# A hand-written order for every engine in the third stage of a fused four-layer network, and eight slots of reciprocals

## The reference, cut to what matters

```python
x = x + L2_attn(layernorm(x))   # 16 heads of 8, window of +-32, softmax, W_o
x = x + L2_ffn(layernorm(x))    # silu(x @ wg.T) * (x @ wu.T) @ wd.T, hidden 384
x = x + L3_attn(layernorm(x))   # 16 heads of 8, rope, latent k and v, causal by pages of 32
x = x + L3_ffn(layernorm(x))    # 8 experts, top 1; the router's part lies in this stage
```

```python
# L3_attn, per head
scores = einsum(q, k) / sqrt(8); scores[masked] = -inf
out = softmax(scores) @ v
```

## Time and profile before

| what | us |
|---|---|
| median of 3 runs | 1353.43 |
| lowest and highest | 1347.26, 1355.87 |
| the profiled execution | 1362.73 |
| span of its instructions | 1360.9 |
| rounds of the third stage from the second `l2f_0` (at 660.7) to the last (at 1127.5) | 76.1, 77.3, 78.7, 78.8, 79.8, 76.1 |
| from the last `l2f_0` to the stage's end at 1245 | 117.5 |

### The profile page before, as it was taken

The page is one execution under the profiler, slowest core; times in us unless marked ns, Lnnn a source line. Parts: engine busy times, 40 slices in busy tenths (PEclk is TensorE's granted clock), DMA queues, the critical chain, the costliest instruction groups (busy, mean ns, idle before and its releaser), DMA issues.

```text
span 1360.9 us, 39674 instructions
## 1 busy us (share of the span) xinstructions
PE 1117.9 (82%) x17027; PEld 805.4 (59%) x17027; DVE 823.8 (61%) x2399; ACT 567.4 (42%) x993; POOL 446.1 (33%) x538
## 2 busy tenths in 40 slices
PE   6999968888875798587888888888888887987895
PEld 4777737777764375354555656556565654553784
DVE  7587765667885122356758586776848575734332
ACT  3322102555452131324373745638274553451342
POOL 3233342344464154213131324133222403112565
PEclk9999979998985899899999999999999998998998
DMA  9455425543040421222112212202221200201784
GB/s 363 165 200 196 180 76 171 168 141 115 26 155 25 111 62 43 58 59 60 50 51 60 59 50 60 60 28 59 60 58 50 61 12 12 56 19 50 194 193 92
DMA packets 85169, 126.08 MB, mean 93 GB/s; under 512 B 14465, under 2 KB 66050, under 8 KB 84578
## 3 DMA queue, kind: packets, MB, share of 16 engines
q1 hardware_dynamic: 68258, 106.47, 24.8%
q0 software_dynamic: 10928, 13.64, 4.2%
q10 hardware_dynamic: 5808, 3.43, 1.0%
HBM read 50.82 MB, written 46.74 MB: 72 GB/s over the span
## 4 chain that ended last, share of the span: by engine, by line
PE 34%; DVE 26%; issue 13%; ACT 12%; POOL 6%; DMA 5%; SPq 1%; another core or an unknown queue 1%; PEldq 1%; ACTq 0%; DVEq 0%; PEld 0%; POOLq 0%
DVE mx L1712 9%; ACT MW L1996 6%; DVE bst L1144 2%; DVE mx L1703 2%; PE ps L996 2%; PE ps L987 2%; POOL xs L2134 2%; DMA MW<-l_moe_dram 2%; PE ps L797 1%; PE ps L988 1%; DVE X L1172 1%; POOL rr L2197 1%; PE ps L1110 1%; POOL rst L2080 1%; PE ps L909 1%
## 5 line engine op out<-in xcount | busy, mean ns | idle before, releaser
L1712 DVE TENSOR_REDUCE mx<-ps 128x2 f32<-128x1024 f32 (+3 forms) x176 | 188.6, 1119 | 30.8 <-PE ps L1033 30.6
L1996 ACT ACTIVATE MW<-ps 128x1024 f32<-128x1024 f32 x160 | 154.4, 1038 | 65.1 <-PE ps L1050 52.8
L2134 POOL DMA_INDIRECT xs<-xr,sidu x96 | 96.1, 1001 | 132.2 <-DVE sidu L1303 95.2
L2077 POOL TENSOR_SCALAR rst<-bmv 128x4 f32<-128x4 f32 x64 | 15.8, 247 | 293.5 <-DVE bmv L1147 292.9
L1065 PE MATMUL ps<-MW,Vp 128*16 128x128 f32 x2560 | 88.1, 279 | 4.6 <-ACT MW L1996 4.0
L1033 PE MATMUL ps<-K,Q 64*128 64x512 bf16 (+3 forms) x512 | 60.0, 303 | 18.2 <-DVE mx L1712 12.0
L1983 ACT ACTIVATE MW<-ps 128x1024 f32<-128x1024 f32 x64 | 63.5, 1026 | 27.1 <-PE ps L958 25.1
L1065 PEld LDWEIGHTS ps<-MW,Vp 128*16 128x16 f32 x2560 | 64.1, 98 | 16.2 <-ACT MW L1996 5.6
L2160 POOL DMA_INDIRECT out_dram<-qf,toku x39 | 60.6, 1555 | 37.1 <-DVE toku L1768 28.2
L1801 ACT COPY XT<-ps 128x512 f32<-128x512 f32 x48 | 28.2, 587 | 97.1 <-PE ps L617 78.7
L1703 DVE TENSOR_REDUCE mx<-ps 128x8 f32<-128x768 f32 x64 | 57.9, 948 | 14.6 <-PE ps L935 14.2
(11 more groups left out here) (377 smaller groups left out, 2676.6 us busy)
## 6 DMA issues: line engine op xcount, KB each, us to landing
xs<-hb SPq DMA_DIRECT2D x52, 528.0 KB, 8.9
MW<-l_moe_dram SPq DMA_DIRECT2D x19, 768.0 KB
MW<-l_moe_dram SPq DMA_DIRECT2D x20, 578.0 KB
Q<-spl SPq DMA_DIRECT2D x48, 128.0 KB
Q<-spm SPq DMA_DIRECT2D x48, 128.0 KB
K<-spl SPq DMA_DIRECT2D x43, 128.0 KB
K<-spm SPq DMA_DIRECT2D x43, 128.0 KB
MW<-l_moe_dram SPq DMA_DIRECT2D x16, 256.0 KB
```

The source lines that it names most:

```text
L1712: V.tensor_reduce(out=mx[1][:, :, s0:s0 + ns, t], in_=p.rearrange("p (e n) -> p e n", e=2)[:, :, 0:ns * nk].rearrange("p e (s k) -> p e s ...
L1996: A.activation(P3[k % 2][:, 1024 * half:1024 * half + 1024], p, ACT.Exp).then_inc(drained[u], 1)
L2134: G.indirect_dma_start(out=xs[L], out_offset=bass.IndirectOffsetOnAxis(ap=sidu[:, 4 * b + t:4 * b + t + 1], axis=0), in_=src[:, t, :], in_ ...
```

## The change

Two edits. `STEPS2` and `lanes(STEPS2, 74.5)` go, and `ORDER2` is written out with `sequences`: one list per engine, in which the n-th appearance of a name is batch n-1. Every (piece, batch) pair of before is in the new lists once and on the same engine; PE's list has 672 entries, DVE's 472, ACT's 320, POOL's 104, SP's 40. The pattern no longer repeats exactly from batch to batch. The slots of the PSUM ring follow PE's new order. Extra matmuls that a piece brings along (`AHEAD_OF`, and the ones in front of the last batch's `l3_m`) stay with their piece. The second edit gives `rden` 8 x 16 columns in place of 4 x 16, so that each of the four `_t` pieces of a batch has a slot of its own; in the old kernel `t0` and `t2` shared one.

```diff
-STEPS2 = [
-    ("l2_get", dict(SP=-130)),
...
-    ("l3t_x", dict(POOL=480.36)),
-]
-ORDER2 = lanes(STEPS2, 74.5)
+ORDER2 = sequences({
+    "PE": """
+        l2a_n l2_q l2_v l2a_n l2_m0 l2_m1 l2_m2 l2_m3 l2_n2 l2_q l2_e0 l2_e1 l2_o0 l2_e2 l2_o1 l2_t0 l2_e3 l2_t1 l2_o2 l2_o3 l2_t2 l2_t3 l2_u l2_j
...
+    """,
+})
-        rden = sb("rden", [128, 4 * H])
+        rden = sb("rden", [128, 8 * H])
-        rdens = [rden[:, 16 * k:16 * k + 16] for k in range(4)]
+        rdens = [rden[:, 16 * k:16 * k + 16] for k in range(8)]
-                    rd = rden[:, :].rearrange("p (t h) -> p t h", t=4)
+                    rd = rden[:, 0:64].rearrange("p (t h) -> p t h", t=4)
             def out_t(key, l, t):
                 u, n, p = unit(key)
-                k = 2 * l + t % 2
+                k = 4 * l + t
```

179 lines of the change are left out of this document (80 added, 99 removed).

## The result

The changed kernel took 1346.2 us (median of 16 runs, 1337.9 to 1353.7) against 1353.6 of before (16 runs). The ratio is 0.9947, with a 95% interval of 0.9925 to 0.9968: **7.2 us less by the ratio (the two medians differ by 7.4), where 20 were forecast**.

What follows compares the result with a forecast made beforehand. No engine is full; how engines wait for one another holds the round. Rounds 13, last maxima 4, ramp 1.2 and 1.5 make 19.7, say 20: 1353.4 to 1333 us; own range 1323 to 1343, overall range 1314 to 1360.

Steps and rivals of the forecast that it cites:

- a round gains 1.2 to 4.6; I take 3: Third-stage rounds: early maxima and an earlier ACT half shorten each round by 1.2 to 4.6 us, taken as 3.
- 0 to 1.5 lost: First half of a round: PE's stall of 0.1 to 2.1 us for the stack costs ACT 0 to 1.5 us.
- The walk to the stack: Stack's last issue at about 929.0, landing 2.3 us later (4.27 by another row); PE at the first maxima at about 931.2.
- The maxima end up to 4.6 earlier: DVE's `l3_m` reductions: 3.8 us from idle time plus 0.8 from the earlier start let them end 4.6 us earlier.
- Rival 1: Path `l2_e0` to `l2_j` and feed-forward sets the round; maxima end early, rounds gain 0 to 1.2; 1345 us; chance 0.26.
- Rival 2: Stack lands too late at the first `l3_m`, stalling PE and ACT; landing near 937 gives 1367 us; chance 0.14.
- ACT half: `l3_e2` ahead of `l3_k` on PE removes ACT's 1.48 us wait at most; taken as 0.8 us.
- Rounds, 13: Five rounds of the kind shown: four gain 3 us each, the one at place 3 gains 1; together 13.
- Last maxima, 4: Batch 7: four maxima ahead of `l3_e8` let DVE, alone the bound, start sooner; 4 us.
- Ramp, 2.7: Ramp: ACT's `l2_p1` of batch 1 moved ahead of exps, 1.2 us; `l2a_n` and `l2_q` of batch 2 earlier, 1.5.
- `l3t_x` at 0 and the reciprocals at 0: Router's indirect DMAs ahead of `l3_n1` lie in POOL's idle, cost nothing; more `rden` slots count 0, 0.1 either way.
- Rival 3, a higher clock: Tighter order keeps PE at full clock in four rounds, 6 to 8 us on top; 1316 us; chance 0.10.

Runs made afterwards that it cites:

- the joined lists: Old and new lists joined at an `l2f_0`; ratios to before: new up to round 0 0.9982, up to round 4 0.9950, rounds 5, 6 and end alone 1.0018.
- e7: Changed kernel with three of twelve 128 KB DMAs left out of layer 3's stack from batch 2 on (result invalid, timing only); 0.9913 of the kernel before.
- e18: The same kernel as e7, measured once more; 0.9880 of the kernel before.
- e17: Changed kernel with three more 128 KB DMAs among layer 3's stack on SP from batch 2 on; 1.0073 of the kernel before.
- e3: Changed kernel with the early maxima put back to their old places in the last round (batch 7) alone; 0.9944 of the kernel before.
- e5: Old table with eight `rden` slots, `l3_e2` ahead of `l3_k` on PE and `l3_p2` ahead of `l2_n1` on POOL; 1.0021 of the kernel before.
- e15: New lists for ramp and first round only, old order from the second `l2f_0` on; 0.9982 of the kernel before.
- e1: Old periodic order with only the second edit, eight slots of `rden`; 1.0002 of the kernel before.
- e9: Old table with eight `rden` slots and `l3t_x` moved ahead of `l3_n1` on POOL; 0.9988 of the kernel before.
- e10: Changed kernel with `l3t_x` put back behind `l3_n1` on POOL in batches 0, 1, 3 and 4; 0.9964 of the kernel before.
- e2: Changed kernel with the early maxima put back behind `l2_q` and `l2_e0` in all seven rounds; 1.0060 of the kernel before.
- e16: The changed kernel itself, measured again on another chip; 0.9947 of the kernel before.
- e12: Changed kernel with `l3_n1` (batches 4, 6) ahead of `l3f_s`, `l3t_x` (batch 2) later, batch 7's first six maxima behind `l3_e9`; 0.9959 of the kernel before.
- e13: New lists up to the sixth `l2f_0`, old order behind it (POOL from `l3f_s` of batch 3); 0.9950 of the kernel before.

## Why the prediction was wrong

**The step that failed** is "a round gains 1.2 to 4.6; I take 3", and in it the assumption that moving the maxima costs the first half almost nothing: "0 to 1.5 lost" at the stall, and `l2_e0` at 940.1 against 939.95. The second half was shortened by 2.6 a round, near the forecast; the first half grew by 1.5 to 1.9 (the table of marks), in good part because PE waits for the stack with `l3_e8` behind it, in four of the six rounds, and in two of these runs at half clock behind that wait. So a round gained 1.7 in the profile (10.0 over six rounds) and about 1.1 by the joined lists, in place of 13 over five. With the last maxima at 0 in place of 4 that is, by the middles of the measurements, the whole difference between 20 and 7. Point by point:

- *The walk to the stack* was right in its times. Last issue 36.2 behind `l2f_0` forecast, 916.73 - 880.71 = 36.0 measured; landing 2.3 forecast, 1.98 measured (918.71 - 916.73). The median row and the Trainium skill's estimate (DMA: Bandwidth & Descriptors, Anatomy of one DMA, which it gives for DMAs issued from GpSimd, where these are issued from SP) held against the row of 4.27; in the other places where PE waited, behind stacks that SP alone issues, the landing was 1.95 to 3.03 behind the last issue. PE came to the place at 36.7 and not at 38.4 as I had walked: the stall was 1.34 in this round, inside my 0.1 to 2.1, but 2.0 to 2.5 in three of the six places and 3.67 in the last round, 13.1 in all.
- *What the stall costs* was too low. I counted "0 to 1.5 lost" and took 3, the middle. In round 4 ACT lost 1.43, but in rounds 1 and 5 it stood 3.75 and 3.61 us, behind waits of 2.00 and 2.19, with PE at a granted clock of 0.50 and 0.54 right behind them. By e7, e18 and e17 each us of wait comes with about one of time. Adding the 13.1 to the 7.2 measured gives 20, the forecast, but that fit is partly luck: the first two waits (2.47 and 2.00) were not varied, and removing the last round's 3.67 together with its early maxima (e3) gained nothing.
- *The maxima end up to 4.6 earlier*: 0.9 in the round shown, and between 2.8 earlier and 0.5 later in the six. They began 2.8 to 8.5 earlier, 7.3 in the round shown. Rival 1 named this sign, DVE's idle time moving behind the first maxima, and its time of 1345 was the nearest. It is half right: the next `l2f_0` follows `l2_j` by 7.4 to 9.6 us in every round, and `l2_e0` was not earlier, as it said; but the way from `l2_e0` to `l2_j` did become shorter, which it left untouched. Rival 2's sign, PE waiting for a DMA into K in front of `l3_m`, was there, at up to 2.2 us in rounds 1 to 6 and 3.67 in the last. Its landing of 934.2 is 41.4 behind `l2f_0`; measured it was 38.0 in round 4, but 41.2 in round 5, which gained 0.8.
- *ACT half*: the wait ahead of `l3_e2` is gone, as forecast (902.80 has none). No gain came of it: e5 has that move, with `l3_p2`, and is no faster, and in the changed kernel the half ends where it ended or later.
- *Rounds, 13*: 10.0 over the six rounds in the profiled execution, about 4.4 by the joined lists. I had counted five; there are six. In the round of place 3 another 1.5 went to POOL's splits beside DVE's normalising (below).
- *Last maxima, 4*: 0 by e3, known to some 5, and by the ends in the profiles. I had counted the sooner start and not that four maxima now stand between the last exps, and that PE waits 3.67 there.
- *Ramp, 2.7*: not shown. e15 gives 2.5 less, but its interval reaches from 5.8 less to 0.8 more, and in the profiles ramp and first round together take 129.4 before, 128.0 in e1, and 130.5 and 130.7 in the changed kernel. The first stack landed at 621.97, which is 4.2 behind SP's last issue and 3.6 behind ACT's, which issues five DMAs of this stack, and not 2.3.
- *`l3t_x` at 0 and the reciprocals at 0*: within the intervals, by e9, e10 and e1. The rows speak for 0.5 to 0.7 a round in favour of `l3t_x` ahead.
- *Rival 3, a higher clock*: no. Stretches at half clock are no rarer than before in rounds 1 to 4, and the first round has more: a granted clock of 0.85 and 0.87 in the changed kernel, 0.97 and 0.95 before and in e1.

What stays open is which moves carry the gain. No group that I took alone does; the early maxima are needed (e2), and the rest may lie in many small moves that I did not separate.

## What to carry to other kernels

When a piece is moved ahead to fill another engine's idle time, look up when its own inputs land, and follow what stands behind it in the same queue. A slack of 8 us had hidden a queue of twelve DMA issues; with the slack used up, the end of that queue set the rounds. Here a stall of 2 us in front of two queued blocks of the bounding engine cost that engine up to 3.75, with the clock at half behind it: charge such a stall at least in full until a row shows otherwise. Walk several rounds, since the one that I walked was the mildest. And compare rounds, not whole profiles: of the 20 us between two profiles 7.6 lay ahead of the changed stage and 4.0 behind it.

## What the runs showed of the hardware

**SP's issues as a bound.** An issue takes 0.60 us of SP (the row of 916.13), and the twelve of a stack from batch 1 on take 8.4 to 9.6 us with their gaps. Three DMAs more moved the landing by some 3 us (waits of 1.40 and 1.34 became 4.45 and 4.13).

**Half clock behind a wait.** Behind the five waits for the stack in batches 1, 2, 4, 5 and 7 the granted clock of the next 3 us is 0.50, 1.00, 1.00, 0.54 and 0.65 in the changed kernel (waits of 2.00, 1.40, 1.34, 2.19 and 3.67) and 0.50, 0.50, 1.00, 1.00 and 0.54 in e16 (waits of 2.02, 2.15, 1.19, 1.70 and 3.83). e7 has 1.00 behind a wait of 2.09 in batch 1, so the length of the wait alone does not decide it. The 32 products of `l3_b` right behind take 1.91 us at half clock and 1.07 at full.

**DVE held by POOL.** In the round of place 3, DVE's four normalising operations took 2.63 us in place of 1.11, just while POOL ran its two subtractions (the rows of 952.79 and 952.57), and PE waited 2.25 for them in the link between `l2_j` and `l2f_0`. The profiles of e12, e13 and e16 have the same 2.63 in the same place, and no other `l2f_n` of the changed kernel has more than 1.28. A second place has it too: the router's product in line 1178 (1197 before), 0.19 us in every batch before, takes 1.03 to 1.09 in four batches now, and at 911.99 it ends at 913.08 where POOL's pair in line 2087 ends at 913.03. The Trainium skill (SBUF — State Buffer, SBUF: two separate sides) says that DVE and GpSimd share one port pair, which one of them holds for a whole instruction, on DVE's side in certain modes or with two inputs in SBUF; the trace agrees, with 1.5 us more beside two operations of 1.15. Which mode DVE ran in no run here shows.

**Gaps in PE's row that nothing releases.** In the second profile of the changed kernel, e16, PE in round 5:

```profile
984.00 0.20 PE L916 MATMUL ps<-K,Q 64*32 64x96 bf16 x1 [0.41 <-issue]
...
985.42 0.72 PE L916 MATMUL ps<-K,Q 64*32 64x96 bf16 x27 [0.43 <-issue]
986.07 5.36 PE L977 MATMUL ps<-W,hb 128*128 128x128 f32 x24
```

The 24 products of the last row took 2.94 in the first profile, without gaps before them, and the first exp of that round came 18.4 behind `l2f_0` in place of 14.0. Gaps over 0.25 us of this kind number 8 to 13 in rounds 1 to 6 in every profile of the three sets in which the kernel before ran at 1359.7 to 1363.7, and 0 to 3 in every profile of the sets in which it ran at 1351.8 to 1353.6. Similar lists have them in similar places. What makes them was not tested. They go with some 9 us of a set's level, and old and new lists seem to be touched alike, since the ratio was 0.9947 in both kinds of set.
